# A layer with attention on one Trainium2 core: the partial sums of the values leave TensorE and ScalarE for DMA and GpSimd

## What is computed

```
x = x + 0.5 * FFN(layernorm(x))
x = x + Attention(layernorm(x))
x = x + 0.5 * FFN(layernorm(x))

Attention(X):
    ctx = X @ We.T
    Q, K, V = heads(X @ Wq.T), heads(X @ Wk.T), heads(X @ Wv.T)
    scores = Q @ K.T * SCALE + 0.1 * (ctx @ ctx.T)
    return (softmax(scores) @ V) @ Wo.T
FFN(x): fp4(silu(fp4(x) @ fp4(w_gate).T) * (fp4(x) @ fp4(w_up).T)) @ fp4(w_down).T
```

## Time and profile before

| | us |
|---|---|
| three runs: median (lowest to highest) | 4039.08 (4036.52 to 4042.34) |
| profiled execution, its own time | 4050.0 |
| its span | 4048.2 |
| busy in the span: PE | 3807.0 (94%) |
| DVE | 3249.4 (80%) |
| ACT | 2490.7 (62%) |
| POOL | 455.4 (11%) |
| DMA: bytes moved, mean rate | 186.52 MB, 46 GB/s |

### The profile page before, as it was taken

How to read it: one execution, slowest core, us unless ns; L and a number is a source line. 1 busy time by engine, 2 the same in 40 slices (tenths; PEclk the granted TensorE clock), 3 DMA queues, 4 the chain that set the end, 5 groups by cost and what they waited for, 6 DMA issues and landing times. The chain is left out here.

```text
span 4048.2 us, 91447 instructions
## 1 busy us (share of the span) xinstructions
PE 3807.0 (94%) x29204; PEld 2213.2 (55%) x29204; DVE 3249.4 (80%) x5168; ACT 2490.7 (62%) x2898; POOL 455.4 (11%) x274
## 2 busy tenths in 40 slices
PE   3998599999999999999999999999999999996698
PEld 2986355555555555555555555555555555553598
DVE  6984588878888888788888887888888878885697
ACT  4663266666666666666666666666666666663365
POOL 4980100000000000000000000000000000000397
PEclk7999699999999999999999999999999999997799
DMA  3004412121212121212121212121212121213200
GB/s 123 0 0 148 106 37 44 38 43 37 45 37 44 37 45 40 41 38 46 38 44 37 44 36 45 36 44 36 45 36 44 36 44 36 45 38 78 87 20 21
DMA packets 316697, 186.52 MB, mean 46 GB/s; under 512 B 195488, under 2 KB 246592, under 8 KB 315872
## 3 DMA queue, kind: packets, MB, share of 16 engines
q1 hardware_dynamic: 315248, 181.27, 20.5%
q10 hardware_dynamic: 1136, 1.08, 0.1%
HBM read 147.75 MB, written 33.82 MB: 45 GB/s over the span
## 5 line engine op out<-in xcount | busy, mean ns | idle before, releaser
L1185 DVE TENSOR_REDUCE tops<-coarse 128x1 f32<-128x512 f32 x4144 | 2681.2, 686 | 588.4 <-PE coarse L1046 484.6
L1161 ACT ACTIVATE probs<-fine 128x1024 f32<-128x1024 f32 x2048 | 1998.4, 1021 | 1018.2 <-PE fine L1065 1018.1
L1076 PE MATMUL o_ps<-probs,vh 128*32 128x512 f32 x8192 | 1092.3, 605 | 0.2 <-ACT probs L1161 0.2
L1055 PE MATMUL fine<-query_a,key_a 64*128 64x512 f32 x4096 | 922.7, 447 | 19.8 <-issue 19.1
L1055 PEld LDWEIGHTS fine<-query_a,key_a 64*128 64x128 f32 x4096 | 388.0, 186 | 929.4 <-ACT probs L1161 750.1
L1046 PE MATMUL coarse<-key_a,max_query 64*128 64x512 f32 x4144 | 834.4, 398 | 44.2 <-DMA key_c<-scratch_c_key 23.4
L1065 PE MATMUL fine<-query_b,key_b 33*128 33x512 f32 x4096 | 818.6, 395 | 0.0
L1061 PE MATMUL fine<-query_c,key_c 64*128 64x512 f32 x4096 | 816.3, 394 | 0.0
L1046 PEld LDWEIGHTS coarse<-key_a,max_query 64*128 64x128 f32 x4144 | 395.0, 187 | 114.5 <-DVE tops L1185 29.7
L1065 PEld LDWEIGHTS fine<-query_b,key_b 33*128 33x128 f32 x4096 | 389.2, 186 | 90.3
L1061 PEld LDWEIGHTS fine<-query_c,key_c 64*128 64x128 f32 x4096 | 389.4, 187 | 84.5
(11 more groups left out here) (157 smaller groups left out, 2326.0 us busy)
## 6 DMA issues: line engine op xcount, KB each, us to landing
query_c<-scratch_c_query SPq DMA_DIRECT2D x258, 128.0 KB, 2.7
max_query<-scratch_q_hi SPq DMA_DIRECT2D x524, 32.0 KB, 1.8
max_query<-scratch_c_query SPq DMA_DIRECT2D x262, 64.0 KB, 2.0
query_a<-scratch_q_hi SPq DMA_DIRECT2D x516, 32.0 KB, 1.8
query_a<-scratch_c_query SPq DMA_DIRECT2D x258, 64.0 KB, 2.0
query_b<-neg_max SPq DMA_DIRECT2D x1032, 0.5 KB, 2.0
query_b<-scratch_q_lo SPq DMA_DIRECT2D x258, 32.0 KB, 2.4
scratch_attended<-result SPq DMA_DIRECT2D x512, 8.0 KB
```

The source lines that it names most:

```text
L1055: pe.matmul(fine[i % 2][:, r, :], key_a[kp][half_rows(r, 0, HALF), cols], query_a[half][half_rows(r, 0, HALF), :], start=True, stop=False)
L1076: last = pe.matmul(o_ps[32 * j:32 * (j + 1), :], vh[kp][:, kt, :], probs[:, kt // 2 % RING, kt % 2, :], start=g == 0, stop=g == NG - 1)
L1161: act.activation(probs[:, i % RING, :, :], fine[i % 2][:, :, :], ACT.Exp).then_inc(probs_ready, 1)
L1185: dve.tensor_reduce(tops[n][:, idx // KB, idx % KB:idx % KB + 1], bank[:, :], AX.X, ALU.max).then_inc(tops_ready, 1)
```

## The change

**The sums.** `sel`, `finish`, `take_result`, `result` and the DRAM buffers for values and sums go. A new class `Sums` holds a resident buffer `at` of all attended values, `ot`, `part` and small tiles. In each step SyncE gathers the row groups 1 to 3 of `ot` by three DMAs of 17 rows (16 values and the sum) into `part`, so that they lie on the partitions of row group 0; GpSimd adds them in three additions of 17 x 512. SyncE copies the row of sums to `few` (16 x 32), VectorE inverts it behind the eighth unit of the step's second half (`INVERT_AFTER`), SyncE saves the inverses to DRAM and loads them back spread over 16 rows, GpSimd multiplies, and SyncE stores the result into `at` in the round after. The exponentials, scores and maxima are as before.

**The order of SyncE's round** becomes: six query DMAs, wait for the multiplied result of two steps ago, four query DMAs, store into `at` and wait until it has landed, gather, wait for GpSimd's additions, copy of the sums, eight DMAs of the maxima, wait for VectorE, save, six query DMAs for the maxima, wait until the save has landed, spread.

**The ends.** Work on maxima past the last step goes; loops over heads keep seven rounds and a written-out last one. The parts of Wo and of the down weights are loaded during the last head into the space of keys that are done with. `output_phase` has no loads of values or scales and no multiplication: ScalarE takes the high part from `at`, GpSimd the low part, VectorE adds and takes the statistics a block later. The last two steps' chains of the sums lie in this stage, and the gate and up weights are loaded behind the last gather.

**The projection**: `x_norm(b + 1)` moves to the start of the body of block b.

The core of the diff:

```diff
-                        if i == NEXT_AFTER - 1 and has_next(b):
-                            x_norm(b + 1)
                         if i == NEXT_AFTER and has_next(b):
                             x_lo(b + 1, 1 - n)
...
+class Sums:
+
...
+    def gather(self, sp, s):
+
+        sp.wait_ge(self.ot_ready, s + 2)
+        for j in range(1, QT):
+            sp.dma_start(self.part[:, j - 1, :], self.ot[32 * j:32 * j + self.ROWS, :]).then_inc(self.gathered, 16)
+
+    def copy_sum(self, sp, s):
+
+        sp.wait_ge(self.sum_ready, s + 2)
+        sp.dma_start(self.few[:, :], self.part[DK:DK + 1, 0, :]).then_inc(self.few_loaded, 16)
+
...
+    def store(self, sp, head, block, stored):
+
+        first = head * DK % P
+        sp.dma_start(self.at[first:first + DK, head * DK // P, block], self.part[0:DK, 0, :]).then_inc(stored, 16)
+
+    def add_parts(self, eng, s):
+
+        eng.wait_ge(self.gathered, self.GATHERS * (s + 1))
+        eng.tensor_tensor(self.part[:, 0, :], self.part[:, 0, :], self.part[:, 1, :], ALU.add).then_inc(self.chain, 1)
+        eng.tensor_tensor(self.part[:, 2, :], self.part[:, 2, :], self.ot[0:self.ROWS, :], ALU.add).then_inc(self.chain, 1)
+        eng.wait_ge(self.chain, 2 * s + 2)
+        eng.tensor_tensor(self.part[:, 0, :], self.part[:, 0, :], self.part[:, 2, :], ALU.add).then_inc(self.sum_ready, 1)
...
+                def step(s, half, finish):
+
+                    sp.wait_ge(probs_ready, P_LEAD + PAIRS * s)
+                    if within(s + 1):
+                        load_operand_a(1 - half, query_a, s + 1, q_loaded)
+                    if finish is not None and finish[0] is not None:
+                        sp.wait_ge(sums.result_ready, s - 1)
+                    if within(s + 1):
+                        load_others(1 - half, s + 1)
+                    if finish is not None:
+                        if finish[0] is not None:
+                            head, block = finish[0]
+                            sums.store(sp, head, slice(block * QB, (block + 1) * QB) if isinstance(block, int) else bass.ds(block * QB, QB), sums.stored)
+                            sp.wait_ge(sums.stored, 16 * (s - 1))
+                        sums.gather(sp, s - 1)
+                        sums.copy_sum(sp, s - 1)
+                    if within(s + 1):
+                        load_max(s + 1, 1 - half)
+                    if finish is not None:
+                        sums.save_inverse(sp, s - 1)
+                    if within(s + 3):
+                        sp.wait_ge(coarse_ready, UNITS // 2 * (s + 2))
+                        load_operand_a(1 - half, max_query, s + 3, mq_loaded)
+                    if finish is not None:
+                        sums.spread_inverse(sp, s - 1)
...
-                        act.wait_ge(fin_ready, F_LEAD + s)
-                    act.activation(ot[:, :], o_ps[:, :], ACT.Copy).then_inc(ot_ready, 1)
+                    act.wait_ge(sums.sum_ready, s + 1)
+                    act.activation(sums.ot[:, :], o_ps[:, :], ACT.Copy).then_inc(sums.ot_ready, 1)
...
```

More of the change, by code:

```diff
@@ L882, in steps, with two_heads @@
             pairs = NQB // 2
[L883 removed]
+            def two_heads(hp):
                 for kp in range(2):
                     u = (hp * 2 + kp) * pairs
[L886 removed]
+                    body(hp, u, 0, kp, last_keys=1 - kp, unless_first=hp if kp == 0 and not isinstance(hp, int) else None, ends=NQB)
                     body(hp, u, 1, kp, last_keys=kp, unless_first=None, ends=NQB - 1)
@@ L892, in steps, with index, within @@
                     body(hp, u + pairs - 1, 1, kp, last_keys=kp, unless_first=None, ends=1)
+            with eng.Fori(0, H // 2 - 1) as hp:
+                two_heads(hp)
+            two_heads(H // 2 - 1)
+        def index(eng, s):
+            return s if isinstance(s, int) else eng.snap(s)
+        def within(s):
+            return not isinstance(s, int) or s < STEPS
         with nc.Block() as block:
@@ L983, in _ @@
                 load_max(0, 0)
[L985 to L991, removed]
-                    sp.dma_start(scratch["sums"][bass.ds(s // NQB, 1), bass.ds(s % NQB * QB, QB)].rearrange("h (j t) -> (h j) t", j=QT),
-                                 result[n][DK:P:32, :]).then_inc(stored[n], 16)
@@ new lines, in _ @@
+                step(0, 0, None)
+                step(1, 1, [None])
+                for head in range(H - 1):
+                    with sp.Fori(0, NQB // 2) as i:
+                        for half in range(2):
+                            block = 2 * i + half
+                            step(sp.snap(head * NQB + block + 2), half, [(head, block)])
+                    if head + 2 < H:
+                        load_keys_a(head % 2, head + 2)
+                        load_keys_b(head % 2, head + 2)
@@ L1031, in _ @@
+                for block in range(NQB - 2):
+                    step((H - 1) * NQB + block + 2, block % 2, [(H - 1, block)])
+                    for dst, src, loaded in reload[block:block + 1]:
+                        sp.dma_start(dst, src).then_inc(loaded, 16)
             @block.tensor
@@ new lines, in body @@
+                    if within(s + 2):
+                        reduce_max(s + 2, half, 0)
+                    if within(s + 1):
+                        max_rows(s + 1, 1 - half)
+                    if within(s + 2):
+                        for idx in range(1, INVERT_AFTER + 1):
+                            reduce_max(s + 2, half, idx)
+                    if unless_first is None:
+                        sums.invert(dve, s - 1)
+                    else:
+                        with dve.If(unless_first):
+                            sums.invert(dve, s - 1)
@@ new lines, in macaron_kernel @@
+        sums = Sums(nc, ctx, sem, scratch["inv_sums"])
+        first_keys = [ctx.enter_context(nc.sbuf_tensor(f"key_{name}0", [P, T // 2], F32R)) for name in "ab"]
+        again, early = {}, []
+        for keys, part in zip(first_keys, ("hi", "lo")):
+            cols = 0
+            for n, (shape, dt), loaded in (("d_" + part, FFN_W["d_" + part], ffn_reload), ("o_" + part, OUT_W["o_" + part], o_reload)):
+                again[n] = keys[:, cols:cols + shape[1] * shape[2]].rearrange("p (a b) -> p a b", a=shape[1])
+                early.append((again[n].bitcast(F32), dram[n], loaded))
+                cols += shape[1] * shape[2]
```

301 lines of the change are left out of this document (123 added, 178 removed).

## The result

| | us |
|---|---|
| before, median (lowest to highest) | 4040.71 (4036.52 to 4050.84), four runs |
| after, median (lowest to highest) | 4589.18 (4586.93 to 4594.10), four runs |
| after / before | 1.1355, interval 1.1331 to 1.1378 |
| profiled execution after: its time, its span | 4594.1, 4592.3 |

The kernel is 549 us slower. The direction was forecast, the size was not: 4368 was expected, and 4589 lies above the range, which ended at 4560.

A forecast was written before the change was run, and what follows sets the result against it. TensorE bounds the kernel before at 25.02 us a step; afterwards SyncE's 27.7 us round would. Summed, 4050 + 386 (attention) - 9 (projection) - 48 (output stage) = 4379 us profiled, hence a median of 4368, range 4160 to 4560.

The forecast's parts named there:

- SyncE becomes the bound: Attention: SyncE's round of 27.7 us, mean 28.2 with keys, exceeds TensorE's 24.7 and sets the step; +386 us.
- One engine for 17 rows: SyncE's gathers: each 17-row transfer uses one DMA engine, 1.68 us each; three end 6.75 us after issue.
- the last term of SyncE's round: SyncE, from issuing the copy of the sums through maxima, save, queries and spread to the loop's end: 9.6 us.
- The sum of the round: SyncE's round in attention: 5.31 + 2.0 + 6.75 + 4.05 + 9.6 = 27.7 us.
- The range: Whole kernel's median time: 4160 to 4560 us, covering the gather's bounds and two slower cases.
- Key loads: SyncE, after 14 heads: six key DMAs add 4.17 us each time to the rounds, 58 us in all.
- What leaves TensorE: Attention step: removing `finish` saves TensorE 0.30 us, from 25.02 to some 24.7; at most 38 us if TensorE stays bound.
- Output stage and projection: Output stage falls from 93.3 to 45 us, -48; seven later projection waits for the normalised block go, -9.1.
- The rival of gathers on all engines: SyncE's gathers land within 3.5 us, round 23.7, TensorE stays the bound: 3966 us, between 3940 and 4020; chance 0.15.
- The clock: TensorE, idling 3.5 us per attention step, drops towards half speed: 4432 us, at worst 4690; chance 0.10.

The follow-up runs named there:

- the pause of TensorE was moved away: Changed kernel, 17 rows, with VectorE's inverse moved to the end of its step (INVERT_AFTER 7 to 15): 4593.19 us, 1.1354 of before.
- The last run: Changed kernel with 32 rows, maxima ahead of the copy, inverse four units later, keys in three parts, half the rounds written out: 3955.43 us, 0.9779 of before.
- With SyncE out of the way: Changed kernel with 32 rows, maxima issued ahead of the copy of the sums, inverse four units later (INVERT_AFTER 11): 4019.81 us, 0.9941 of before.

## Why the prediction was right and wrong

- **SyncE becomes the bound.** Right. SyncE waits for ScalarE and TensorE next to nothing (3.3 us), and when the pause of TensorE was moved away, the time stayed.
- **One engine for 17 rows.** Right in mechanism and size: 6.53 us to the landing where 6.75 were forecast, one engine busy, and 18 or 32 rows undo it. With the additions it came to 10.44 instead of 10.80.
- **The step that failed** is the last term of SyncE's round, from the copy of the sums to the end of the loop, 9.6 us in the sum. In the round shown above it took 2032.78 - 2021.50 = 11.28 us, and in the mean of the 106 rounds that carry no loads of keys or weights 10.9. The issues came out about as forecast: 0.57 + 5.09 + 0.44 + 3.07 + 0.38 = 9.55 in the round shown, where the 3.07 hold a gap of 0.56. I had put 0.4 for the waits between them and for the loop, from no row, and in this round these gaps are 1.73: 0.48 between the save and the queries of the maxima, 0.92 between the spread and the next round's first query, and smaller ones. The last run shows where most of them come from: where rounds are written out with fixed step numbers, both gaps are 0.04 in the median, so they belong to rounds in a loop, whose step numbers are worked out as it runs.
- **The sum of the round.** In the mean of the same 106 rounds the parts are, with the forecast behind each: queries up to the store 5.8 (5.31), store 2.35 (2.0), gathers and additions 10.44 (10.80), the rest 10.9 (9.6). A round is 29.47 us long instead of 27.71, and the 1.76 more, over 124 rounds, are the 218 us. So 1.3 of it is the last term; the queries and the store, both too short in the sum, add 0.8, and the gathers take 0.36 off. The rounds vary from one to the next: the one shown is long in the store and the last term.
- **The range** had bounds for the gather and for GpSimd, which were the questions that I saw, and none for the gaps between SyncE's issues. They are the larger part of what lay outside.
- **Key loads.** Right. The forecast charged 4.17 us after 14 heads. The 14 rounds with them took 34.04 us in the mean, 4.57 more than the others.
- **What leaves TensorE** was forecast as 0.30 us per step, from 25.02 to 24.7. With SyncE out of the way the median step was 24.62, and the median step of the kernel before is 24.75, so 0.13 is nearer. That 24.7 came close is luck: the 25.02 is a mean, and seven long steps of some 30 us at the back edge of the loop over two heads are in it.
- **Output stage and projection.** Right: 43.4 us for 45; for the projection's 9, 12.0 by the first copy and 5 to 14 by the run of it alone.
- **The rival of gathers on all engines** gave 3966 for a round that fits. With 32 rows the gathers did land within 3.5 us (3.33), and the time was 4213: the condition that I gave wasn't enough, since the rest of the round was longer than the sum had it: rounds without key loads took 26.4 us in the mean, where the rival had 23.7.
- **The clock** fell as the rival said, but by SyncE's waits it set nothing: a round begins with a wait for ScalarE's exponentials, which TensorE feeds, and this wait came to 3.3 us in all. No run has the long round without the low clock.

## What to carry to other kernels

Where one engine issues transfers, waits and further transfers in one program, its round is a resource like TensorE's time: add up the issues, the waits, and the gaps between them from a timeline, and compare with the step before moving work onto it. The gaps alone were 1.7 us of a round here. Give a transfer a number of rows that divides evenly, here 18 or 32 rather than 17, even at the price of more bytes. Put what the next step needs ahead of a wait for something that only this step's end needs, and then look at the loop that this order makes.

## What was not expected of the hardware

VectorE's additions in the output stage take four times as long beside GpSimd. VectorE's timeline of the last step's additions, with the mean of the second FFN at its end, and GpSimd's beside it:

```profile
4297.54 0.68 DVE L880 TENSOR_TENSOR part<-part 17x512 f32<-17x512 f32 x1 [14.16 <-DMA part<-ot]
4298.15 2.86 DVE L881 TENSOR_TENSOR part<-part,ot 17x512 f32<-17x512 f32 x1
4301.04 2.72 DVE L883 TENSOR_TENSOR part<-part 17x512 f32<-17x512 f32 x1
...
4331.26 0.22 DVE L331 TENSOR_TENSOR mean<-stats 128x32 f32<-128x32 f32 x1 [0.56 <-PEq L1286]
```

```profile
4298.07 2.40 POOL L1320 TENSOR_TENSOR o_at_lo<-at,o_at_hi 128x1024 fp32r<-128x1024 f32 x1 [4.10 <-ACT o_at_hi L1310]
4300.88 2.35 POOL L1320 TENSOR_TENSOR o_at_lo<-at,o_at_hi 128x1024 fp32r<-128x1024 f32 x1 [0.41 <-ACT o_at_hi L1310]
```

The same shape takes 0.68 us with GpSimd idle until near its end, and 2.86 and 2.72 while GpSimd has subtractions of two SBUF operands, which end at 4300.47 and 4303.23; VectorE's end 0.5 us behind them. It cost some 4 us once, in a stage of 43. (The profile's spans on GpSimd are rough.) The Trainium skill ("GPSIMD Engine Reference", section "1. Specifications") says that GpSimd shares its SBUF interfaces with VectorE, with contention for VectorE instructions with two SBUF inputs. The trace agrees, but no run was made to separate the two, so the cause is not shown. In the attention GpSimd's additions cost nothing of the kind: the maxima, which read PSUM, have a mean of 0.68 us, as before (0.69).

What stays open: the six long steps at the back edge of the loop over two heads, of which the kernel before, whose loop goes round once more, has seven (in the fastest version TensorE stands still for 2.4 to 3.0 us in each, and the profile shows nothing that it waits for), and why a store into `at` lands in 1.4 us in one round and in 2.5 in another.
